# Attention logits in lanes by products of bfloat16 pieces, and the bucket fetch at the head of TensorE's step

## What is computed

```python
e = x_l[src] + x_r[dst] + (ea @ W_e).reshape(-1, H, C)
e = jnp.where(e > 0, e, NEG_SLOPE * e)
logits = jnp.einsum('ehc,hc->eh', e, att)
m = jax.ops.segment_max(logits, dst, num_segments=N)
a = jnp.exp(logits - m[dst])
denom = jax.ops.segment_sum(a, dst, num_segments=N)
alpha = a / denom[dst]
out = jax.ops.segment_sum(x_l[src] * alpha[..., None], dst, num_segments=N)
```

## Time and profile before

| | us |
|---|---|
| median of 3 runs | 2756.62 (2756.12 to 2776.38) |
| profiled execution | 2753.45 |
| its span, first to last instruction | 2751.4 |
| PE busy in the span | 2373.4 (86%) |
| DVE busy | 1881.6 (68%) |
| ACT busy | 1417.1 (52%) |
| POOL busy | 1272.7 (46%) |

### The profile page before, as it was taken

One profiled execution on the slowest core, in us unless ns is written; L12 is line 12 of the kernel. 1 busy time (PEld: TensorE's weight loads), 2 busy tenths in 40 slices (PEclk: granted clock), 3 DMA queues, 4 the chain that ended last, 5 costly groups with the idle time before them and its releaser, 6 DMA issues. The chain is left out here.

```text
span 2751.4 us, 59642 instructions
## 1 busy us (share of the span) xinstructions
PE 2373.4 (86%) x16218; PEld 1902.1 (69%) x16218; DVE 1881.6 (68%) x6983; ACT 1417.1 (52%) x4559; POOL 1272.7 (46%) x1302
## 2 busy tenths in 40 slices
PE   5985869998876998767999999999999999249994
PEld 3884537876643565435999999999999998126663
DVE  8785799999876333355666666666666665874445
ACT  1781004444422222245888888888888886621110
POOL 1346777777763774134444444444444440005441
PEclk9786679999987999888999999999999998569997
DMA  5303334434433345134222222222222243162224
GB/s 176 100 29 104 102 97 101 104 101 104 106 115 102 105 160 184 39 108 119 72 72 72 73 72 73 71 73 72 72 72 72 72 72 110 53 219 70 66 60 157
DMA packets 252542, 261.41 MB, mean 95 GB/s; under 512 B 143396, under 2 KB 202783, under 8 KB 251844
## 3 DMA queue, kind: packets, MB, share of 16 engines
q0 software_dynamic: 57344, 151.11, 19.7%
q1 hardware_dynamic: 191572, 103.26, 13.3%
q10 hardware_dynamic: 3312, 3.28, 0.3%
HBM read 198.46 MB, written 59.06 MB: 94 GB/s over the span
## 5 line engine op out<-in xcount | busy, mean ns | idle before, releaser
L2293 POOL DMA_INDIRECT l_rows<-xl_tab,l_ra x454 | 442.6, 975 | 571.4 <-DMA l_ra<-rec_a 461.8
L2434 DVE CUSTOM_DVE_ANT_0 l_junk<-l_ps_lb,l_pen 128x256 bf16<-128x256 f32 x908 | 331.3, 421 | 282.3 <-PE l_ps_lb L2396 280.8
L1014 POOL DMA_INDIRECT room_a<-h_tab,c_rec x432 | 439.4, 1017 | 136.9 <-issue 77.7
L1061 PE MATMUL c_ps<-room_a 128*128 128x256 f32 x864 | 310.0, 448 | 83.1 <-DVE room_a L1343 49.6
L1061 PEld LDWEIGHTS c_ps<-room_a 128*128 128x128 f32 x864 | 161.1, 210 | 181.6 <-DVE room_a L1343 128.3
L1031 ACT ACTIVATE s_cum<-iota_f,c_row_f 128x128 f32<-128x128 f32 x391 | 122.8, 389 | 311.3 <-PE c_ps_s L1099 204.9
L2366 PE MATMUL l_ps_ag<-l_val,l_hot 128*128 128x260 f32 x908 | 256.5, 405 | 0.1
L2331 ACT ACTIVATE l_val<-l_rows,l_val 128x64 f32<-128x64 f32 x908 | 241.7, 337 | 7.4
L2321 ACT ACTIVATE room_a<-room_a,l_cexp x908 | 241.3, 345 | 1.3 <-issue 1.3
L2356 PE MATMUL l_bank_l<-g_att_d,l_rz 128*128 128x4 f32 x1816 | 240.5, 253 | 0.4 <-ACT l_rz L2343 0.4
L2396 PE MATMUL l_ps_lb<-ident,l_ls 128*128 128x128 f32 x1816 | 235.2, 273 | 0.0
(11 more groups left out here) (596 smaller groups left out, 5466.6 us busy)
## 6 DMA issues: line engine op xcount, KB each, us to landing
m_w<-in_L_ffn_w SPq DMA_DIRECT2D x16, 1024.0 KB, 7.9
rec_a<-room_a SPq DMA_DIRECT2D x114, 102.0 KB
l_ra<-rec_a SPq DMA_DIRECT2D x227, 51.0 KB, 2.1
e_w<-in_L_ffn_W SPq DMA_DIRECT2D x16, 512.0 KB, 12.1
l_rows<-xl_tab,l_ra POOLq DMA_INDIRECT x454
room_a<-h_tab,c_rec POOLq DMA_INDIRECT x432, 2.8
xrr_tab<-q_xrr SPq DMA_DIRECT2D x25, 256.0 KB, 2.0
f_xrr<-xrr_tab SPq DMA_DIRECT2D x5, 1280.0 KB, 13.2
```

The source lines that it names most:

```text
L1014: pool.indirect_dma_start(rows[:, u, :], None, K["h_tab"], bass.IndirectOffsetOnAxis(ap=rec[:, n % RSLOTS, k, 0:1].bitcast(I32), axis=0)). ...
L1061: pe.matmul(ps[s % NB][:, :], hot[:, u, :], rows[:, s % RU, :], start=True, stop=True).then_inc(s_agg, 1)
L2293: pool.indirect_dma_start(rows[:, u, j, :], None, K["xl_tab"], bass.IndirectOffsetOnAxis(ap=ra[:, u, j, A_SRC:A_SRC + 1].bitcast(I32), axi ...
L2434: dve.tensor_tensor_reduce(junk[:, h, :], ps_lb[:, h, :], pen[:, v3, :], 1.0, -3.0e38, ALU.add, ALU.max, tmax[:, v3, h:h + 1]).then_inc(S[ ...
```

## The change

The eight float32 transposes go. VectorE, after `ls`, makes two further pieces: `lsp` holds for each edge and head the logit, the logit less its upper half, and that less its upper half again. TensorE transposes the upper halves of the three (12 columns) by two bfloat16 transposes into `ps_lt`, behind the aggregation and ahead of z; VectorE copies them to `lt` (12 x 256) behind the new maximum; and behind z four bfloat16 products of 256 columns, one to a head, with `pick` as weights (ones in the three rows of that head, in all 128 columns) sum the three pieces into `ps_lb`. `pick` is built once by three VectorE operations at the stage's start, and TensorE waits for it there. The bucket number that z needs is now fetched at the head of TensorE's step.

```diff
--- before.py
+++ after.py
@@ -2220,7 +2220,11 @@
         pen = t("pen", [P, U, SUPER], F32)
         stk = t("stk", [STK, U, SUPER], BF16)
         rz = t("rz", [P, 2, 2, SUPER], F32)
-        ls = t("ls", [P, U, SUB, HEADS], F32)
+        NPC = 3
+        lsp = t("lsp", [P, U, SUB, NPC, HEADS], F32)
+        ls = lsp[:, :, :, 0, :]
+        lt = t("lt", [NPC * HEADS, 2, SUPER], BF16)
+        pick_f, pick = t("pick_f", [NPC * HEADS, HEADS], F32), t("pick", [NPC * HEADS, HEADS, P], BF16)
         arg = t("arg", [P, U, SUB, HEADS], F32)
         junk = t("junk", [P, HEADS, SUPER], BF16)
         tmax, mnew, dm, cexp = (t(n, [P, U, HEADS], F32) for n in ("tmax", "mnew", "dm", "cexp"))
@@ -2235,14 +2239,15 @@
         ps_stk = bank_t[0:STK, P:2 * P].bitcast(BF16)
         bank_l = c.enter_context(nc.psum_tensor("l_bank_l", [P, 512], F32))
         ps_lg = bank_l[:, 0:SUB * HEADS].rearrange("p (j h) -> p j h", j=SUB)
+        ps_lt = bank_l[0:NPC * HEADS, P:2 * P].bitcast(BF16)
         ps_z = [c.enter_context(nc.psum_tensor(f"l_ps_z{k}", [P, 2, SUPER], F32)) for k in range(2)]
         ps_lb = c.enter_context(nc.psum_tensor("l_ps_lb", [P, HEADS, SUPER], F32))
         ps_ag = [c.enter_context(nc.psum_tensor(f"l_ps_ag{k}", [P, 512], F32)) for k in range(2)]
         ps_md = [ps[:, AGW + AUX:AGW + AUX + SUB * HEADS].rearrange("p (j h) -> p j h", j=SUB) for ps in ps_ag]
         s_ra = [sem(f"l_ra{k}") for k in range(U)]
         s_rows = K["dma_sems"]("l_rows", U)
-        names = ("hot stk_ps hot_c stk_c z rz lg ls lb tm mn mr ml dm mst c md arg a val1 val ag sc acc pb"
-                 ).split()
+        names = ("hot stk_ps hot_c stk_c z rz lg ls ls1 ls2 lt ltc lb tm mn mr ml dm mst c md arg a val1 val ag sc acc "
+                 "pb pick").split()
         S = {n: sem("l_" + n) for n in names}
         LAST = 5
         WORDS = 40
@@ -2345,7 +2350,10 @@
 
         @block.tensor
         def _(pe):
+            pe.wait_ge(S["pick"], 4)
+
             def step(s, u, i, ctx):
+                b = early(pe, ctx[s - 1]) if live(s, 1, SUPERS) else None
                 if live(s, 2, SUPERS):
                     r, v = s - 2, (u - 2) % U
                     pe.wait_ge(S["rz"], r + 1)
@@ -2370,9 +2378,16 @@
                                        ra[:, v, j, A_AUX:REC_A].bitcast(BF16)[:, 0:AUX],
                                        start=(j == 0), stop=(j == SUB - 1))
                     mm.then_inc(S["ag"], 1)
+                if live(s, 2, SUPERS):
+                    r, v = s - 2, (u - 2) % U
+                    pe.wait_ge(S["ls2"], r + 1)
+                    wait(pe, S["ltc"], r)
+                    for j in range(SUB):
+                        mm = pe.transpose(ps_lt[:, j * P:(j + 1) * P],
+                                          uppers(lsp[:, v, j, :, :].rearrange("p k h -> p (k h)")), K["ident_b"][:, :])
+                    mm.then_inc(S["lt"], 1)
                 if live(s, 1, SUPERS):
                     r, v = s - 1, (u - 1) % U
-                    b = early(pe, ctx[s - 1])
                     pe.wait_ge(S["hot_c"], 2 * r + 1)
                     pe.wait_ge(S["stk_c"], r + 1)
                     wait(pe, S["rz"], r - 1)
@@ -2389,12 +2404,10 @@
                     mm.then_inc(S["z"], 1)
                 if live(s, 2, SUPERS):
                     r, v = s - 2, (u - 2) % U
-                    pe.wait_ge(S["ls"], r + 1)
+                    pe.wait_ge(S["ltc"], r + 1)
                     wait(pe, S["tm"], 4 * r)
                     for h in range(HEADS):
-                        for j in range(SUB):
-                            mm = pe.transpose(ps_lb[:, h, j * P:(j + 1) * P],
-                                              ls[:, v, j, h:h + 1].to_broadcast([P, P]), ident[:, :])
+                        mm = pe.matmul(ps_lb[:, h, :], pick[:, h, :], lt[:, v % 2, :], start=True, stop=True)
                     mm.then_inc(S["lb"], 1)
                 if live(s, 0, SUPERS):
                     pe.wait_ge(S["hot"], s + 1)
@@ -2419,6 +2432,17 @@
 
         @block.vector
         def _(dve):
+            k0, k1, k2 = (ident[0:NPC * HEADS, k * HEADS:(k + 1) * HEADS] for k in range(NPC))
+            dve.tensor_tensor(pick_f[:, :], k0, k1, ALU.add).then_inc(S["pick"], 1)
+            dve.wait_ge(S["pick"], 1)
+            dve.tensor_tensor(pick_f[:, :], pick_f[:, :], k2, ALU.add).then_inc(S["pick"], 1)
+            dve.wait_ge(S["pick"], 2)
+            dve.tensor_copy(pick[:, :, :], pick_f[:, :].rearrange("p (h o) -> p h o", o=1)
+                            .to_broadcast([NPC * HEADS, HEADS, P])).then_inc(S["pick"], 2)
+
+            def high(v):
+                return v.bitcast(BF16).rearrange("p j (h two) -> p j h two", two=2)[:, :, :, 1]
+
             def step(s, u, i, ctx):
 
 
@@ -2440,6 +2464,12 @@
                     r, v = s - 2, (u - 2) % U
                     dve.wait_ge(S["lg"], r + 1)
                     dve.tensor_tensor(ls[:, v, :, :], ps_lg, rows[:, v, :, D:ROW_L], ALU.add).then_inc(S["ls"], 1)
+                    dve.wait_ge(S["ls"], r + 1)
+                    dve.tensor_tensor(lsp[:, v, :, 1, :], lsp[:, v, :, 0, :], high(lsp[:, v, :, 0, :]), ALU.subtract
+                                      ).then_inc(S["ls1"], 1)
+                    dve.wait_ge(S["ls1"], r + 1)
+                    dve.tensor_tensor(lsp[:, v, :, 2, :], lsp[:, v, :, 1, :], high(lsp[:, v, :, 1, :]), ALU.subtract
+                                      ).then_inc(S["ls2"], 1)
                 if live(s, 0, SUPERS):
                     dve.wait_ge(s_ra[u], 16 * i + 16)
                     dve.tensor_tensor(hot[:, u, :, :],
@@ -2450,6 +2480,11 @@
                     dve.wait_ge(S["tm"], 4 * r3 + 4)
                     wait(dve, S["mst"], r3)
                     dve.tensor_tensor(mnew[:, v3, :], tmax[:, v3, :], m, ALU.max).then_inc(S["mn"], 1)
+                if live(s, 2, SUPERS):
+                    r, v = s - 2, (u - 2) % U
+                    dve.wait_ge(S["lt"], r + 1)
+                    wait(dve, S["lb"], r - 1)
+                    dve.tensor_copy(lt[:, v % 2, :], ps_lt).then_inc(S["ltc"], 1)
                 if on4:
                     dve.wait_ge(S["a"], r4 + 1)
                     dve.tensor_tensor(val[:, v4 % 2, 0:SUB - 1, :, 0:HC],
```

## The result

The changed kernel took 2789.43 us in the median of 9 runs (2785.46 to 2809.79), the kernel before, run beside it, 2756.2 (9 runs). The ratio is 1.0135, 95% interval [1.0113, 1.0156]. I had forecast 2723 us and at most 2748. The profiled execution took 2787.74 us, 34 more than before's.

What follows compares the result with a forecast made beforehand. TensorE bounds the attention stage; afterwards a loop through VectorE and TensorE would, its pieces summing to 4.41 us a step against 4.56. (4.56 - 4.41) x 222 = 33 us off 2756.6 gives 2723 us, range 2700 to 2748.

Steps and rivals of the forecast that it cites:

- TensorE's own work: TensorE's work in a steady step: 4.56 - 0.87 + 0.55 = 4.24 us; as the bound a rival, 2685 us, chance 0.04.
- these six: The four bfloat16 lane products and two bfloat16 transposes added on TensorE each step, taken at 0.55 us together.
- The loops: Two cyclic chains of waits through a step: TensorE with VectorE, 4.41 us, forecast to bound; TensorE with ScalarE, 4.35.
- ScalarE's loop: From z through ScalarE's relu, logits' products and transposes back to z: 4.35 us a step, hidden by the longer chain.
- Per step to whole: The saving per steady step times 222 steps: (4.56 - 4.41) x 222 = 33 us off the whole time.
- VectorE's wait for the lane products: VectorE's idle time each step before the lane products, forecast to fall from 1.25 to about 0.6 us.
- The new VectorE work: Two subtractions, 0.38 us in sum, and a copy out of PSUM, 0.45: 0.83 a step, within 1.25 idle.
- The sequencer stops at a wait: TensorE's instruction sequencer does not run on behind a wait: 0.20 us, not 0.11, from the transposes' load to z's.
- Gathers: Slower rival: VectorE's two subtractions wait for GpSimd's gathers, 0.40 us a step, 4.81 us and 2812; chance 0.07.
- The move of the fetch: Bucket fetch moved to the head of TensorE's step, hidden under running products: costed at nothing, 0.3 us a step uncovered.
- The rivals: Sequencer running ahead, 2710 us, chance 0.20; TensorE alone, 2685, 0.04; costlier hand-overs, 2745, 0.19; waiting for gathers, 2812, 0.07.

Runs made afterwards that it cites:

- e9: e5 with VectorE's copy of `ps_lt` to `lt` moved behind `dm`; 2721.23 us, ratio to before 0.987.
- e1: The changed kernel with the logits' transposes zero-padded to 128 weight columns and the lane products to 128 contracting rows; 2742.85 us, ratio to before 0.9953.
- e4: The changed kernel with the bucket fetch put back ahead of z, now behind the transposes' wait; 2824.71 us, ratio to before 1.0235.
- e12: The kernel before with only the bucket fetch moved to the head of TensorE's step; 2754.65 us in one execution.
- e5: e1 with the two logits' transposes placed between the two halves of z; 2789.48 us, ratio to before 1.0122.
- e7: The changed kernel with 30 extra 512-column TensorE products ahead of the stage's first step and 16 behind that step's transposes; 2797.93 us.

## Why the prediction was wrong

- **TensorE's own work: the step that failed.** "No row has only 12 contracting rows or 12 output rows. Bounds for these six: 0.28 us together if they took half of the above, 0.55 if as much. I take 0.55, since the stream of columns is the same." The upper bound was none. The six take 0.55, but they stand in two groups of another shape than their neighbours, and the four switches add 0.37 (from the table, against 108, 109, 25, and the 56 of e9 for transposes to z: 0.095 + 0.091 + 0.088 + 0.094), and what lies just behind them some 0.04 (0.011 + 0.011 + 0.020 + 0.003). 4.24 + 0.37 + 0.04 = 4.65, measured 4.651, more than the 4.56 that it started from. The bound from above lacked the question what a product of a shape that no row shows does to those beside it. I had also priced the six by their distances within a group ("0.11 each"), where nothing of a switch can be seen.
- **The loops: the size right, their order not.** e1, where the switches are gone, has a step of 4.411, and I had 4.41. But TensorE's load follows `rz` there by 0.05, the bare hand-over, and `lsp` by 0.07, 0.02 more than it: ScalarE's loop, which I had at 4.35, sets the 4.41 (from the transposes' load to z's it is 0.17 and not the 0.11 that I took for this loop), and VectorE's is some 0.02 shorter. That 4.411 meets 4.41 to the third digit is luck. In the changed kernel both are hidden: the transposes' load starts 0.17 behind `lsp`, and but for one of 172 steps TensorE has no wait in the steady part that names another engine.
- **Per step to whole: too simple.** e1 has my step and not my time. From its first lane products to its last it takes 1007.1 us, before 1027.1: 20 less, not 33. Its first three steps last 20.4 us, 8.9 more than before's 11.50, and a twentieth of its steps is longer than 4.57. My sum had nothing for the run-up, where the same chain is worked through at half clock. And of these 20 the whole shows 14 (2742.85 against 2757.19): e1's lane products also begin 7 us later, at 1290.4 and not 1283.3. Where that comes from is open; the start of the stage differs by some us from kernel to kernel.
- **VectorE's wait for the lane products** fell from 1.25 to 0.84 us and not to 0.6: VectorE's new work took its share, and the longer step gave some back.
- **The new VectorE work:** the subtractions last 0.17 each and start 0.20 apart, as taken; the copy 0.28, where I took 0.45.
- **The sequencer stops at a wait: right** (e4), its price behind the transposes half of the 0.3 that I gave. That it stops at the wait for `mlow` too, I did not see.
- **"Gathers": no.** The two subtractions have means of 170 and 172 ns over 172 steps in which GpSimd is busy 0.42 of the time (84.20 of 200). 199 of these 344 begin while a gather runs, with a mean of 168 ns, and none begins more than 0.28 us behind the start of the operation ahead. The rule of the Trainium skill, "SBUF — State Buffer", section "Who interferes with whom", by which they would wait for a whole gather, is not borne out for these gathers.
- **The move of the fetch, costed at nothing: right** for the kernel before (e12, 4.561) and for the changed one, where the sum of products alone gives the step. In e5 it is not covered.
- The rivals missed it too: TensorE's own work as the bound was among them, but at 4.24, and with a chance of 0.04.

## What to carry to other kernels

Before a product is made small, look which shape of weights stands before and behind it: here a group with 12 or 64 rows or columns between full ones cost some 0.1 us on going in and as much on coming out, more than the work saved, and padding it with zeros to 128 gave it back. An operation whose input comes later must be moved behind whatever is queued after it, on its own engine and in the chain of the engines that wait for those. Work of the sequencer is hidden only as long as the wait ahead of it ends before the queue runs dry, so after each edit ask again which wait that is. And a bound "as much as the nearest row" is a bound only for a thing among its like.

## What the runs showed of the hardware that I had not expected

- Products of 12 and of 64 rows or columns behave alike at a switch, 96 and 128 alike: 200 to 204 ns against 108 or 109 from start to start, where the ones behind or ahead have 256 columns. The load itself is hardly shorter: mean 92 ns for 12x128 and 85 for 128x12, 97 for 128x128.
- TensorE counts as busy for all of 200.00 us in the changed kernel, though it loses 0.41 us of 4.65 in each step: busy products hide the switches, and only the idle time of the loads (PEld, "issue") and the distances of starts show them.
- A kernel whose TensorE waits 0.66 us before the transposes of its first steps fell back to 1.2 GHz there, 5 us behind the last of 46 dense products of 512 columns (e7), and stayed there for 30.8 us in which it was busy for 29.28 of 30.60.
- TensorE's sequencer stops at a wait: the first register operation behind the transposes' wait starts 0.05 us after the subtraction that is waited for, in 167 steps of e4, whether TensorE is idle or not.
